# Attention inputs of pairs 1 to 31: loaded turned from DRAM and normalised in that layout, in place of products with the identity

## The reference, cut to what matters

```python
xn = layernorm(ctx)                # over the 256 features of each token
ln = layernorm(layernorm(x))       # normalised once as input of the layer, once more inside
q = ln @ Wq                        # 256 -> 16 heads of 64
k, v = split(concat([xn, ln], tokens) @ Wkv)
w = softmax(q k^T / 8)             # 128 latents by 256 keys, per head
x = x + (w v) @ Wo
```

## Time and profile before

| | |
|---|---|
| three runs | 3171.97 us median, 3169.43 to 3172.02 |
| profiled execution | 3171.49 us, its span 3169.8 us |
| attention | from the start to about 1650 us |
| experts | about 1650 to 2700 us |
| alignment and convolution | the rest |
| busy over the span | PE 91%, DVE 75%, ACT 56%, POOL 63% |

### The profile page before, as it was taken

One profiled execution on the slowest core, in us unless ns is written; L12 is line 12 of the kernel. 1 busy time (PEld: TensorE's weight loads), 2 busy tenths in 40 slices (PEclk: granted clock), 3 DMA queues, 4 the chain that ended last, 5 costly groups with the idle time before them and its releaser, 6 DMA issues. The chain is left out here.

```text
span 3169.8 us, 61556 instructions
## 1 busy us (share of the span) xinstructions
PE 2871.4 (91%) x21070; PEld 2473.1 (78%) x21070; DVE 2375.1 (75%) x5003; ACT 1759.9 (56%) x4520; POOL 2006.3 (63%) x1983
## 2 busy tenths in 40 slices
PE   6999999999999999999979999999999943179897
PEld 5888888888888888888868888888888831057675
DVE  5767777677776777777647877878778659889997
ACT  5666666666766666666643333332333326089997
POOL 4888888888888888888853333343333310069887
PEclk9999999999999999999989999999999965589999
DMA  8665655566566665666651111121211260001111
GB/s 216 114 114 108 115 109 115 112 111 117 109 111 117 111 117 105 111 112 113 111 130 58 48 59 60 48 75 44 70 53 51 68 113 1 8 27 47 48 34 41
DMA packets 704757, 272.16 MB, mean 86 GB/s; under 512 B 606168, under 2 KB 667328, under 8 KB 704448
## 3 DMA queue, kind: packets, MB, share of 16 engines
q1 hardware_dynamic: 704448, 268.23, 40.6%
HBM read 120.16 MB, written 13.73 MB: 42 GB/s over the span
## 5 line engine op out<-in xcount | busy, mean ns | idle before, releaser
L843 POOL COPY attention_probT<-attention_planesT 128x1024 uint16<-128x1024 uint16 x512 | 677.7, 1369 | 180.1 <-PE attention_turns L421 102.4
L528 ACT ACTIVATE attention_prob<-attention_turns,attention_neg_max 128x256 f32<-128x256 f32 x1024 | 467.6, 481 | 224.4 <-DVE attention_neg_max L681 214.7
L1434 POOL TENSOR_TENSOR experts_hidden_lo<-experts_weighed,experts_hidden_hi 128x512 fp32r<-128x512 f32 x192 | 254.9, 1328 | 531.4 <-ACT experts_hidden_hi L1187 531.4
L834 POOL COPY attention_planes<-attention_prob 128x1024 uint16<-128x1024 uint16 x512 | 526.6, 1059 | 20.9 <-ACT attention_prob L528 20.9
L681 DVE TENSOR_REDUCE attention_neg_max<-attention_turns 128x2 f32<-128x512 f32 x512 | 317.7, 682 | 176.9 <-PE attention_turns L406 176.8
L382 PE MATMUL attention_turns<-kv_hi,wkv 128*128 128x512 f32 x1024 | 375.0, 407 | 0.0
L1187 ACT ACTIVATE experts_hidden_hi<-experts_weighed 128x512 fp32r<-128x512 f32 x192 | 121.4, 632 | 404.1 <-DVE experts_weighed L1324 404.1
L350 PE MATMUL attention_turns<-wkv,kv_hi 128*128 128x512 f32 x1024 | 315.5, 389 | 1.9 <-ACT attention_prob L528 1.9
L421 PE MATMUL attention_turns<-attention_probT,attention_v 128*64 128x128 f32 x4096 | 255.6, 278 | 3.1 <-issue 3.1
L697 DVE TENSOR_TENSOR attention_turns<-attention_turns,attention_attT_lo 128x512 f32<-128x512 f32 x128 | 139.9, 1093 | 152.0 <-DMA attention_attT_lo<-inverse_rows 150.3
L517 ACT COPY attention_v<-attention_turns 128x512 f32<-128x512 f32 x256 | 150.4, 589 | 184.5 <-PE attention_turns L350 184.5
(11 more groups left out here) (297 smaller groups left out, 8596.4 us busy)
## 6 DMA issues: line engine op xcount, KB each, us to landing
attention_attT_lo<-inverse_rows SPq DMA_DIRECT2D x256, 128.0 KB, 3.0
experts_spread<-shares SPq DMA_DIRECT2D x256, 128.0 KB, 3.0
attention_ctx<-in_ctx SPq DMA_DIRECT2D x32, 256.0 KB, 3.2
attention_planesT<-attention_planes SPq DMA_TRANSPOSE x512, 3.2
experts_far_ctxT<-in_ctxT SPq DMA_DIRECT2D x32, 256.0 KB, 3.4
weights_ctx<-in_ctx SPq DMA_DIRECT2D x16, 512.0 KB, 3.8
out<-conv_x_out SPq DMA_DIRECT2D x15, 512.0 KB, 2.8
x_all<-in_x SPq DMA_DIRECT2D x7, 1024.0 KB, 9.1
```

The costliest lines, as they stand in the source:

```text
L528: made = act.activation(prob[n % 2][:, h, :], bank_of("s", 2 * n + e)[:, m * 256:(m + 1) * 256], ACT.Exp, bias=neg_max[:, n % 2, 2 * e + m ...
L834: pool.tensor_copy(planes[n % 2][:, g, :, :], words.rearrange("p (c b) -> p b c", b=2)).then_inc(planes_made, 1)
L843: pool.tensor_copy(words.rearrange("p (c b) -> p b c", b=2), planesT[:, g, :, :]).then_inc(joined, 1)
L1434: pool.tensor_tensor(hid_lo[n % 3][:, :], weighed[n % 2], hid_hi[n % 3][:, :].bitcast(F32), ALU.subtract).then_inc(hid_split, 1)
```

## The change

Pair 0 is still turned by PE. For pairs 1 to 31 a new input `inT` in DRAM holds context and x of each pair already turned (features on partitions), 512 KB per pair, 4 KB in a row for each partition; SP loads it into `kv_full`, which is now double-buffered. The statistics are still made from the unturned tiles, once: the scale of the twice normalised x is worked out from one variance, var(1 + eps) + eps². POOL writes mean and scale into columns, SP stores them to DRAM (8 numbers per token) and loads them back spread over all 128 partitions (`norm_row`, 512 KB), and DVE subtracts and multiplies in place, two TENSOR_TENSOR of 128x512 per sequence. ACT then reads `kv_full` from SBUF where it read a PSUM bank.

```diff
 def sp_program(sp):
             def load_ctx(p):
-                if p:
-                    sp.wait_ge(turned_in, 2 * p)
+                if p == 1:
+                    sp.wait_ge(turned_in, 2)
+                elif p:
+                    sp.wait_ge(stats_made, p)
...
+            def store_norms(q):
+                sp.wait_ge(rstd_made, q + 1)
+                sp.dma_start(norm_rows[q % 2].rearrange("e t c -> t e c"),
+                             norm_cols[:, :, :].rearrange("p (e c) s -> p e (c s)", e=2)).then_inc(norms_stored, 16)
+
+            def load_norms(q):
+                sp.wait_ge(norms_stored, 16 * q)
+                if q == 1:
+                    sp.wait_ge(turned_in, 2)
+                else:
+                    sp.wait_ge(normed, 2 * q - 1)
+                sp.dma_start(norm_row[:, :, :, :, :].rearrange("p e t c s -> p (e t c s)"),
+                             norm_rows[q % 2:q % 2 + 1].rearrange("o e t c -> o (e t c)").broadcast_to([P, 8 * TOK])
+                             ).then_inc(inputs_loaded, 16)
+
+            def load_turned(q):
+                if q >= 2:
+                    sp.wait_ge(v_made, PER_PAIR * (q - 1))
+                sp.dma_start(kv_full[q % 2][:, :, :, :, :], inT[q]).then_inc(inputs_loaded, 16)
...
             for n in range(WV, WO):
                 load_weight(n)
+            load_turned(1)
             for n in range(2, FREE_LOADS):
                 load_x(n)
...
                 if u < ROUNDS:
+                    if u and not i and p + 1 < PAIRS:
+                        load_turned(p + 1)
+                    store_inverses(u)
                     if i == 3 and p + 2 < PAIRS:
-                        load_ctx(p + 2)
-                    store_inverses(u)
+                        store_norms(p + 2)
                     for g in range(2):
                         turn_planes(2 * u, g)
+                    if i == 1 and p + 2 < PAIRS:
+                        load_ctx(p + 2)
+                    if i == 3 and p + 2 < PAIRS:
+                        load_norms(p + 2)
+                    if not u:
+                        store_norms(1)
+                        load_norms(1)
 def pe_program(pe):
-                if late_input(u) is not None:
-                    turn_inputs(late_input(u))
 def act_program(act): (split_inputs)
-                view = bank_of("in", b)[:, :].rearrange("p (k c t) -> p k c t", k=KD, c=2)
-                act.wait_ge(turned_in, b + 1)
+                full = kv_full[p % 2][:, :, :, e, :]
+                if p:
+                    view = full
+                    act.wait_ge(normed, b)
+                else:
+                    view = bank_of("in", b)[:, :].rearrange("p (k c t) -> p k c t", k=KD, c=2)
+                    act.wait_ge(turned_in, b + 1)
...
-                    if b:
-                        act.wait_ge(kv_split, 2 * b - 1 + k)
 def dve_program(dve):
+            def norm_turned(b):
+                p, e = divmod(b, 2)
+                dve.wait_ge(inputs_loaded, 32 * p)
+                full = kv_full[p % 2][:, :, :, e, :]
+                mean, scale = (norm_row[:, e, :, :, s].rearrange("p t c -> p c t").unsqueeze(1).broadcast_to([P, KD, 2, TOK])
+                               for s in range(2))
+                dve_step(dve, dve.tensor_tensor(full, full, mean, ALU.subtract))
+                dve.tensor_tensor(full, full, scale, ALU.mult).then_inc(normed, 1)
...
                 if u + 1 < ROUNDS:
                     low_k(n + 2)
                     low_q(u + 1)
-                    if u and not i and following_pair:
-                        norm_ctx(following_pair)
                     low_k(n + 3)
-                if not u:
-                    norm_x(1)
-                    norm_ctx(1)
-                if not i and following_pair:
-                    measure_latents(following_pair)
-                if i == 1 and following_pair:
-                    norm_c(following_pair)
-                if measured is not None and u:
-                    measure_x(measured)
-                    measure_ctx(measured)
+                if u == 1:
+                    norm_turned(2)
+                if u and not i and p + 1 < PAIRS:
+                    norm_turned(2 * p + 2)
+                if i == 1 and p + 1 < PAIRS:
+                    norm_turned(2 * p + 3)
+                if i == 2 and p + 2 < PAIRS:
+                    measure(p + 2)
+                    context_norm(p + 2)
 def pool_program(pool):
+            def norm_columns(p):
+                pool.wait_ge(stats_made, p + 1)
+                if p >= 2:
+                    pool.wait_ge(norms_stored, 16 * (p - 1))
+                pool.tensor_copy(norm_cols[:, :, 0], mv[:, :, 0])
+                pool.tensor_scalar(var_eps[:, 0:4:2], mv[:, 0:4:2, 1], EPS, None, ALU.add)
+                pool_step(pool, pool.tensor_scalar(var_eps[:, 1:4:2], mv[:, 1:4:2, 1], 1.0 + EPS, EPS * EPS, ALU.mult,
+                                                   ALU.add))
+                pool.tensor_tensor(norm_cols[:, :, 1], var_eps[:, :], half[:, :], ALU.pow).then_inc(rstd_made, 1)
...
-                if i == 3 and p + 2 < PAIRS:
-                    inverse_std(p + 2, 0, 4)
-                if not i and p + 1 < PAIRS:
-                    inverse_std(p + 1, 1, 2)
+                if i == 2 and p + 2 < PAIRS:
+                    norm_columns(p + 2)
```

More of the change, by code:

```diff
@@ L93, in __init__ @@
         with ExitStack() as held:
+            tiles(held, ("before_kv_full", [3 * KD * INNER + 4 * KD * TOK], F32))
+            self.kv_full, = tiles(held, ("kv_full", [KD, 2, 2, TOK], F32))
+        with ExitStack() as held:
             self.gate_raw, self.up_raw, x, xT = tiles(
@@ L487, in split_inputs @@
                 for k in range(KD):
-                    if b:
-                        act.wait_ge(kv_split, 2 * b - 1 + k)
                     for c in range(2):
-                        made = act.activation(kv_full[k][:, c, :], view[:, k, c, :], ACT.Identity,
+                        made = act.activation(full[:, k, c, :], view[:, k, c, :], ACT.Identity,
                                               scale=cols[:, 2 * c, k:k + 1], bias=cols[:, 2 * c + 1, k:k + 1])
@@ L494, in split_inputs @@
                     act.wait_ge(kv_scaled, 2 * b + k + 1)
-                    act.activation(kv_hi[p % 2][:, k, :, e, :], kv_full[k][:, :, :], ACT.Copy).then_inc(kv_high, 1)
+                    act.activation(kv_hi[p % 2][:, k, :, e, :], full[:, k, :, :], ACT.Copy).then_inc(kv_high, 1)
             def high_q(g):
@@ L596, in dve_program, with normalise, stats @@
         def dve_program(dve):
-            def pair(p):
-                return ([x_all[:, 2 * p + e, :] for e in range(2)], [ctx_sb[:, e, :] for e in range(2)],
-                        [lat[:, e, :] for e in range(2)])
-            def stats(tiles, out):
+            def normalise(outs, tiles, means, scales):
+                for out, t, mean, scale in zip(outs, tiles, means, scales):
+                    made = dve.tensor_scalar(out, t, mean, scale, ALU.subtract, ALU.mult)
+                return made
+            def stats(tiles):
                 for n, t in enumerate(tiles):
@@ L757, in dve_program @@
                 p, i = divmod(u, QUADS)
-                measured = 1 if not u else p + 2 if i == 3 and p + 2 < PAIRS else None
-                following_pair = p + 1 if p + 1 < PAIRS else None
                 if u < ROUNDS:
```

132 lines of the change are left out of this document (54 added, 78 removed).

## The result

The changed kernel takes 3183.73 us (median of 20 runs, 3175.77 to 3189.03), the kernel before 3175.99 us on the same chips (20 runs, 3169.05 to 3182.65): ratio 1.0023, 95% interval 1.0015 to 1.0031. It is slower by 0.2%, where 3128 us were forecast. The profiled execution took 3179.04 us, 7.6 more than the one before: 7.7 in rounds 3 to 121, 3.1 at the start, and 3.3 less behind round 121, where the traces of all kernels lie within 5 us.

A forecast was written before the change was run, and what follows sets the result against it. PE was taken to bound the kernel, at a floor of 12.07 us a round. 3171.5 - 27.3 (turns) - 21.7 (stalls) + 6 (misses) = 3128.5, said as 3128 us; range 3116 to 3158.

The forecast's parts named there:

- what was charged for misses: Rounds missing the narrow cover behind DVE's normalising: 0.2 us a pair, 30 x 0.2 = 6 us added.
- POOL issues four small instructions a pair as before, in one place instead of two: nothing: Step on bank ring, ACT and POOL's small work: POOL's norm instructions were forecast to cost nothing.
- Removed from PE: On PE, 62 turned sequences go at 0.44 us each: 27.3 us gained, covered by no other engine's work.
- removed from DVE's path: Both normalisations leave the stretch before low_k(n + 3), so stalls behind i = 0 vanish: 0.70 x 31 = 21.7 us gained.
- Added on DVE: norm_turned's TENSOR_TENSOR, 1.09 us each, wait for POOL's copies and make row_max 2.2 us late; called the deciding part.
- The lateness is just covered, with 0.2 us to spare: After i = 0, PE's second k product and next low parts still come in time despite row_max 2.2 us late.
- The first rival: All hidden: the strided operand on DVE costs nothing (0.69 us), PE runs at its floor, 3122 us; chance 0.22.
- Added on SP: New loads and a column store per pair, some 0.55 us an issue; the inverses' load may be late by 0.8 us.
- 0.8 is within what the freed 4.1 us cover: In i = 3 the spread load delays the inverses (3.8 against 3.0 us); time freed on DVE absorbs it.
- The third rival: DVE waits for kv_full's late load ahead of row_max; landing 7.8 us instead of 3.8 gives 3227 us; chance 0.08.
- The start: Before the steady rounds: up to 1.5 us gained, up to 4.2 lost to 1 MB more queued; taken as 0.
- The second rival: Locks: DVE's TENSOR_TENSOR hold POOL up until it ends the rounds, 1.2 us a pair, 36 us, 3158; chance 0.18.

The follow-up runs named there:

- e1: The changed kernel with POOL's norm_columns(p + 2) moved behind low_inputs in round i = 2, nothing else; 3158.96 us, ratio 0.9951 to the kernel before.
- e2: The changed kernel with norm_turned's four TENSOR_TENSOR on 2 elements in place of 512, inputs not normalised; 3158.63 us, one run.
- e5: e1 with norm_turned's four TENSOR_TENSOR on 2 elements, inputs not normalised; 3140.78 us, ratio 0.9903 to the kernel before.
- e9: e5 without the store of mean and scale columns and their 512 KB spread load for pairs 2 to 31; 3131.85 us, ratio 0.9865 to the kernel before.
- e3: e1 with pair 1's column store issued ahead of the first turning of planes in round 0; 3156.73 us, ratio 0.9941 to the kernel before.
- e4: e1 with mean and scale read from neighbouring places, so normalised with wrong numbers; 3142.64 us, ratio 0.9903 to the kernel before.
- e11: e3 with each sequence's subtraction left in place and its multiplication moved behind the next round's maxima; 3160.07 us, ratio 0.9959 to the kernel before.
- e8: e6 with rows stored so mean and scale lie in neighbouring places, 1024 pieces of 4 bytes per pair; 3301.24 us, ratio 1.0422 to the kernel before.
- e6: e1 with the 512 KB load of norm_row moved behind the load of the inverses; 3172.15 us, ratio 0.9993 to the kernel before.

## Why the prediction was wrong

The forecast was 1424.3 + 6 = 1430.3 us for the rounds 3 to 121, and nothing for the start. Measured were 1478.2, and a start later by 3.1 (70.89 against 67.75). The 47.9 us of the rounds are these, each the difference of two traces. The first two causes act on the same wait, and what each is worth hangs on which is taken away first, so both orders are given:

| cause | us | from | us, the other order | from |
|---|---|---|---|---|
| POOL's columns ahead of the low part | 26.5 | after 1478.2, e1 1451.8 | 13.0 | e2, e5 |
| length of the two normalising instructions beside POOL | 12.1 | e1, e5 1439.7 | 25.5 | after, e2 1452.7 |
| the rows' store and spread load | 11.9 | e5, e9 1427.8 | 11.9 | the same |
| floor 12.10 instead of 12.07 | 3.5 | 118 x 0.03 | 3.5 | the same |
| less what was charged for misses | -6.0 | the prediction | -6.0 | the same |

Together the first two are 38.5 us; neither is shown to be the larger. Each difference is uncertain by some 5 us, by which the traces of e1 and e3 differ, and two rounds alone, 32 and 112, hold 6.8 of the 11.9. The ratios bear the sizes out: 23, 15 and 12 us for the first three in the first order. By place, i = 3 holds most of the loss: it is 1.41 us over the floor, and i = 0, 1 and 2 are 0.11, 0.20 and 0.02 over it.

**The step that failed** is "POOL issues four small instructions a pair as before, in one place instead of two: nothing". The count was right; the place was not asked about. `norm_columns` stands in front of the one POOL product of the pair on which PE's next round depends. PE waits for it in round i = 3, which took 13.51 us where the prediction had 12.07. The trace of the kernel before invited the question. In its round from 814.58 on the earlier trace rows, POOL, then PE:

```profile
816.08 0.73 POOL L827 TENSOR_TENSOR kv_lo<-attention_kv_full,kv_hi 128x256 fp32r<-128x256 f32 x1 [1.02 <-ACT kv_hi L495]
817.16 0.73 POOL L827 TENSOR_TENSOR kv_lo<-attention_kv_full,kv_hi 128x256 fp32r<-128x256 f32 x1 [0.35 <-ACT kv_hi L495]
```

```profile
818.11 0.50 PE L382 MATMUL attention_turns<-kv_hi,wkv 128*128 128x512 f32 x1
```

The low part ended at 817.89 and PE wanted it at 818.11, 3.5 us into the round: 0.2 to spare, in every round of the kind. POOL's own room was larger, since it had stood idle for 1.02 and 0.35 us until ACT's high parts came. What room it had in the changed kernel is told by the round from 921.30: had the four instructions stood behind, the low part could have begun at 922.5 and ended 1.4 later, at 923.9, and PE was ready for it at 924.90. That is 1.0 to spare, an estimate from these rows; in e5 it is 1.02 at the median. 1.8 us were put in front of it, and 0.8 remain as a stall, which e2 has as 0.77. The prediction asked for DVE and SP what is queued behind each step, and for POOL it did not.

**The same step, second half.** The long instructions on DVE make POOL late in front of that product too: with the columns behind it, e1 has only 0.68 to spare at the median, and PE waits in five rounds. In the changed kernel this adds 0.64 to the 0.77. "i = 3 has nothing on DVE and recovers" looked at DVE alone. The charge of 0.2 us a pair was right for the rounds it was made for (0.20 in i = 1, 0.02 in i = 2) and left out i = 3.

**Removed from PE** and **removed from DVE's path** were right: no turns, and round i = 0 without PE's wait before the scores; e9, which has no rows' transfers and hardly any normalising, shows that all four rounds then run at the floor and that 42.7 us (1470.5 less 1427.8) of the 46.2 forecast for these 118 rounds were there.

**Added on DVE.** The size was right, 1.06 to 1.07 us alone for a forecast of 1.09, and so was what follows in i = 0: 2.2 us late, at +3.2 of the next round (+3.35 in the sample). "The lateness is just covered, with 0.2 us to spare" held nearly, as the charge above. The first rival (0.69 us each) is ruled out by the change and by e4, which makes it true and gains 12 us in the rounds.

**Added on SP.** "0.8 is within what the freed 4.1 us cover" held in the changed kernel, where i = 0 is only 0.11 us over the floor. It no longer holds once i = 3 is short. The spread load also delays the issue, and the 128 KB behind it land in 4.3 us at the median and up to 6.0 (e5), where 2.9 were usual; with the store this costs 11.9 us. The third rival looked for a late transfer at `kv_full`, where the landing was 4.2 us (3.8 forecast) and DVE waited only 33.8 us in all. The late transfer was the one that the prediction had passed.

**The start.** -1.5 to +4 held 3.1 barely, and by luck: six other kernels with the same start are 4.2 to 5.7 us later than the kernel before. What was overlooked is SP standing for its own store, with the turning of planes queued behind it. POOL's join at 56.07 waited 8.40 us for these planes, and PE before the first weighing of round 2 10.72 us, against 7.04 in e3:

```profile
58.73 3.68 PE L457 MATMUL attention_turns<-attention_probT,attention_v 128*64 128x128 f32 x32 [10.72 <-issue]
```

**The second rival** (locks, 3158) had the right engine and a true cost, 36 us in its count and 12 to 25 by the table, but not where it falls: POOL was late for one product, and its rounds were not too full. It still idles over 200 us.

**Open.** The twelve products of L473 take 1.53 us a round in all the new versions against 1.49 before, which makes the floor 12.10. Their means are 282 to 289 ns against 281 to 282; no run tested why. The remaining excess of 0.15 in i = 3 of e1 was not pursued.

## What to carry to other kernels

An in-order engine has a due time for each thing that it makes; before an instruction is put in front of one, however small, read in the trace when the product ended, when it was wanted, and what the engine itself waited for before it. Here 1.8 us of four small instructions turned a gain of 0.5% into a loss of 0.2%, and exchanging two calls brought it back. Where two causes end in one wait, take them away in both orders: here each was worth 26 us alone and 12 to 13 after the other.

A large transfer delays the small one queued behind it. And an operand that an engine reads at a distance should be laid out plain where that costs nothing, but not by a store in pieces of 4 bytes.

## What the runs showed of the hardware

- The same DVE TENSOR_TENSOR of 128x512 takes 0.69 us with plain operands and 1.06 with one whose elements lie 16 bytes apart (e4).
- Beside POOL's copies it takes 1.39 and 1.76 us in the mean, and the copies grow from 1045 to 1181 ns. A two-element one, 0.16 us alone, takes 0.47 and 0.81 there (e2). With one of the two moved to another place, other copies grew (e11).
- A store of 4 KB as 1024 pieces of 4 bytes in place of 256 of 16 cost some 4 us a pair, in transfers of others that came behind it (e8 against e6).
- A load of 128 KB issued right behind one of 512 KB spread over the partitions landed in 4.4 us at the median, and in 3.1 with the large one behind it (e1 against e6).
